# Scattering layer 2's expert results by token instead of gathering them by slot

## The reference

```
xn = _layernorm(x, axis=-1)
s = _L2_attn_ref(xn, ...)
g = _silu(_L2_ffn_ref(xn, ...))
x = x + s * g

def _L2_ffn_ref(x, ...):            # 32 experts, 4 for each token, H = 128
    scores = jax.nn.softmax(logits, axis=-1)
    topk_scores, topk_idx = jax.lax.top_k(scores, TOPK)
    topk_scores = topk_scores / jnp.clip(topk_scores.sum(axis=-1, keepdims=True), 1e-12, None)
    h = jax.nn.silu(jnp.einsum('nd,ehd->neh', flat, gate_w)) * jnp.einsum('nd,ehd->neh', flat, up_w)
    expert_out = jnp.einsum('neh,edh->ned', h, down_w)
    sel = jnp.take_along_axis(expert_out, topk_idx[:, :, None], axis=1)
    out = (sel * topk_scores.astype(flat.dtype)[:, :, None]).sum(axis=1)
    out = out + jax.nn.silu(flat @ sgate_w.T) * (flat @ sup_w.T) @ sdown_w.T
```

## Time and profile before

| | |
|---|---|
| median of 3 runs | 3026.65 us (3012.79 to 3027.65) |
| profiled execution | 3031.52 us |
| its span, first to last instruction | 3029.9 us |
| mean granted clock of PE | 0.854 of full speed |
| busy: PE, DVE, ACT, POOL | 2294.3, 1649.9, 1244.2, 726.5 us |
| layer 2's expert tiles, first row load to the next block | 2323.8 to 2505.55 us |
| `between_layers` | 2505.55 to about 2790 us |
| layer 3's `linear_attention` and projection | 2826.2 to 2890.4 us |
| layer 3's expert tiles, `finish` | 2890.4 to the end |

### The profile page before, as it was taken

How to read it: one execution, slowest core, us unless ns; L and a number is a source line. 1 busy time by engine, 2 the same in 40 slices (tenths; PEclk the granted TensorE clock), 3 DMA queues, 4 the chain that set the end, 5 groups by cost and what they waited for, 6 DMA issues and landing times. The chain is left out here.

```text
span 3029.9 us, 44630 instructions
## 1 busy us (share of the span) xinstructions
PE 2294.3 (76%) x15583; PEld 1330.6 (44%) x15600; DVE 1649.9 (54%) x3303; ACT 1244.2 (41%) x1898; POOL 726.5 (24%) x874
## 2 busy tenths in 40 slices
PE   3487788883599999989750399999998884776486
PEld 1255555552334444444340134444444772344275
DVE  2467676761187756657138277777772441544202
ACT  0234444422156656566520046555665440232043
POOL 0143434443010101100000132323221116450423
PEclk9588898886699999999855599999998996796588
DMA  9000000002002111110000302121212991110065
GB/s 258 1 2 2 2 2 2 2 2 64 31 14 61 35 43 31 56 27 27 1 1 11 92 25 75 48 70 48 70 52 94 314 303 49 31 37 3 28 225 179
DMA packets 135515, 183.14 MB, mean 60 GB/s; under 512 B 26329, under 2 KB 108458, under 8 KB 130190
## 3 DMA queue, kind: packets, MB, share of 16 engines
q1 hardware_dynamic: 95235, 135.53, 15.1%
q0 software_dynamic: 13696, 32.02, 3.3%
q10 hardware_dynamic: 26400, 13.13, 1.5%
HBM read 127.86 MB, written 52.21 MB: 59 GB/s over the span
## 5 line engine op out<-in xcount | busy, mean ns | idle before, releaser
L1691 DVE TENSOR_REDUCE a_mpart<-a_mx 128x1 f32<-128x512 f32 (+3 forms) x1216 | 741.8, 657 | 293.3 <-PE a_mx L1462 157.1
L1605 ACT ACTIVATE a_prob<-a_st 128x1024 f32<-128x1024 f32 (+3 forms) x768 | 607.5, 812 | 489.8 <-PE a_st L1488 367.1
L1462 PE MATMUL a_mx<-a_ka,a_qa 96*128 96x512 bf16 (+3 forms) x1536 | 429.2, 339 | 33.8 <-DVE a_mpart L1691 17.0
L1485 PE MATMUL a_st<-a_qa,a_ka 96*128 96x512 bf16 (+3 forms) x1536 | 416.5, 334 | 27.2 <-ACT a_prob L1605 21.4
L1503 PE MATMUL a_acc<-a_prob,a_v_aug 128*9 128x512 f32 (+3 forms) x3072 | 323.5, 497 | 0.0
L1462 PEld LDWEIGHTS a_mx<-a_ka,a_qa 96*128 96x128 bf16 x1536 | 141.3, 99 | 321.4 <-DVE a_mpart L1691 174.1
L1389 POOL DMA_INDIRECT x_rows<-l_xn,l_slots x128 | 125.5, 980 | 403.5 <-ACT a_prob L1605 393.5
L1488 PE MATMUL a_st<-w_mask_t,identb 128*128 128x128 bf16 x1024 | 208.3, 223 | 0.0
L1485 PEld LDWEIGHTS a_st<-a_qa,a_ka 96*128 96x128 bf16 x1536 | 146.1, 99 | 132.8 <-ACT a_prob L1605 37.4
L2053 PE MATMUL t_psu<-t_xsT,t_w 128*128 128x128 f32 x960 | 149.5, 290 | 22.9 <-DMA t_w<-in_l_experts 13.4
L1465 PE MATMUL a_mx<-w_mask_q,identb 128*128 128x128 bf16 x768 | 164.8, 224 | 0.0
(11 more groups left out here) (451 smaller groups left out, 4115.8 us busy)
## 6 DMA issues: line engine op xcount, KB each, us to landing
t_w<-in_l_experts SPq DMA_DIRECT2D x160, 192.0 KB, 4.0
t_w<-in_l_experts SPq DMA_DIRECT2D x40, 514.0 KB
a_qa<-q_parts_dram SPq DMA_DIRECT2D x96, 192.0 KB
a_ka<-k_parts_dram SPq DMA_DIRECT2D x96, 192.0 KB
x_rows<-zeros SPq DMA_DIRECT2D x25, 512.0 KB, 6.7
t_xs<-x_rows ACTq DMA_DIRECT2D x40, 256.0 KB, 4.2
y_rows<-t_y POOLq DMA_DIRECT2D x40, 256.0 KB
q_parts_dram<-a_parts SPq DMA_DIRECT2D x24, 256.0 KB
```

What stands on the lines that cost most here:

```text
L1462: ins = pe.matmul(to, qa[G % NQ][:, h0 + k, qi * P:(qi + 1) * P], ka[G % NQ][:, h0 + k, lo:hi], start=not masked_first, stop=k == per - 1 ...
L1485: ins = pe.matmul(to[:, lo:HALF], ka[G % NQ][:, h, j * P:(j + 1) * P], qa[G % NQ][:, h, ch * HALF + lo:(ch + 1) * HALF], start=True, stop= ...
L1605: act.activation(prob[:, v % NP_, 2 * pair:2 * pair + 2, lo:HALF], sring[s % 2][:, :, lo:HALF], ACT.Exp, scale=1.0 if alibi else scale).th ...
L1691: dve.tensor_reduce(mpart[:, G % 2, h0:h0 + per, qi, piece], slot[:, 0:per * width].rearrange("p (k w) -> p k w", k=per), X, ALU.max).then ...
```

## The change

Row numbers travel with layer 2's rows, too. `x2_rows` gets the column D, `y2_rows` is laid out by token (row 4 * token + k) with 160 tiles of spare rows behind it for unused slots. The expert tiles of layer 2 scatter each tile's results to these rows as those of layer 3 do, four indirect DMAs a half; the number copies of both layers go from DVE to POOL, one half ahead of the half's scatters, into a tile that holds the numbers of all tiles; ACT's loads of rows stand one tile before the end of a half and wait for that copy. The attention of layer 2 adds 1 to the numbers on POOL before the scatters of k = 1, 2, 3 of each sequence. `between_layers` reads the four results of a token as 2 KB in a row, by 16 plain DMAs of SP, 512 KB each, in place of 128 gathers. The projection of the last sequence moves into the block of its attention. The cores of the parts:

```diff
-                        sp.dma_start(x3_rows.rearrange("(i p) d -> p i d", p=P)[:, :, D], row_id[:], allow_slow_non_contiguous=True
-                                     ).then_inc(ids_filled, 16)
                         sp.wait_ge(loaded, 16 * len(loads))
+                        for rows, ids in zip((x2_rows, x3_rows), no_token):
+                            sp.dma_start(rows.rearrange("(i p) d -> p i d", p=P)[:, :, D], ids[:], allow_slow_non_contiguous=True
+                                         ).then_inc(ids_filled, 16)
...
+                            if k and t == 0:
+                                ids = seqs[b].rows[:, :, D]
+                                pool.wait_ge(placed[b], 16 * NT * k)
+                                pool.tensor_scalar(ids, ids, 1.0, None, ALU.add).then_inc(numbered, 1)
+                                pool.wait_ge(numbered, (TOPK - 1) * b + k)
                             pool.indirect_dma_start(x2_rows, bass.IndirectOffsetOnAxis(x_slots[:, k, b * NT + t:b * NT + t + 1], 0),
-                                                    seqs[b].xn[:, t], None, bounds_check=x2_rows.shape[0] - 1).then_inc(placed[b], 16)
+                                                    seqs[b].rows[:, t], None, bounds_check=x2_rows.shape[0] - 1).then_inc(placed[b], 16)
...
+                    def keep_ids(it, half):
+                        at = it * body + half * hb
+                        pool.wait_ge(x_loaded[half], 16 * (it + 1))
+                        pool.tensor_copy(ids[:, at:at + hb], xs[:, half, :, D]).then_inc(ids_kept, 1)
+
                     def store(it, half):
                         pool.wait_ge(y_out, it * pairs + (half + 1) * hb // 2)
-                        if base is None:
-                            pool.dma_start(half_tiles(y_view, it, half), y[:, half]).then_inc(y_stored[half], 16)
-                        else:
-                            for j in range(hb):
-                                pool.indirect_dma_start(y_rows, bass.IndirectOffsetOnAxis(ids[:, half, j:j + 1], 0), y[:, half, j], None,
-                                                        bounds_check=y_rows.shape[0] - 1).then_inc(y_stored[half], 16)
-
-                    if base is None:
-                        with pool.Fori(0, iters) as it:
-                            for half in range(2):
-                                store(it, half)
-                    else:
-                        for it in range(iters):
-                            for half in range(2):
-                                pool.wait_ge(ids_kept, 2 * it + half + 1)
-                                store(it, half)
+                        pool.wait_ge(ids_kept, 2 * it + half + 1)
+                        for j in range(hb):
+                            at = it * body + half * hb + j
+                            pool.indirect_dma_start(y_rows, bass.IndirectOffsetOnAxis(ids[:, at:at + 1], 0), y[:, half, j], None,
+                                                    bounds_check=y_rows.shape[0] - 1).then_inc(y_stored[half], 16)
+
+                    for half in range(2):
+                        keep_ids(0, half)
+                    for it in range(iters):
+                        for half in range(2):
+                            if it + 1 < iters:
+                                keep_ids(it + 1, half)
+                            store(it, half)
...
-                            if ahead and base is not None and k % hb == hb - 1:
+                            if ahead and k % hb == hb - 2:
                                 act.wait_ge(ids_kept, 2 * it + k // hb + 1)
                                 load(it + 1, k // hb)
...
-                    def keep_ids(it, half):
-                        wait(dve, y_stored[half], it * stores)
-                        dve.wait_ge(x_loaded[half], 16 * (it + 1))
-                        dve.tensor_copy(ids[:, half], xs[:, half, :, D]).then_inc(ids_kept, 1)
...
-                    sp.wait_ge(ids_filled, 16)
+                    view = y2_rows[0:TOPK * BATCH * T].rearrange("(b t p k) d -> b p t (k d)", b=BATCH, p=P, k=TOPK)
+                    for e in order:
+                        if e[0] == "gather":
+                            _, b, q = e
+                            if at[e] >= NB:
+                                sp.wait_ge(summed, at[e] - NB + 1)
+                            sp.dma_start(back[:, at[e] % NB], view[b, :, tiles_of(q)]).then_inc(back_s[at[e] % NB], 16)
 
                 @block.gpsimd
                 def _(pool):
                     pool.memset(v[:, :, D:D + 1], 1.0).then_inc(ones_s, 1)
-                    for e in order:
-                        if e[0] == "gather":
-                            _, b, q = e
-                            k_at = at[e]
-                            if k_at >= NB:
-                                pool.wait_ge(summed, k_at - NB + 1)
-                            for t in range(PER):
-                                for k in range(TOPK):
-                                    fetch(pool, back[:, k_at % NB, k, t], y2_rows, slots[:, k], b * NT + q * PER + t, back_s[k_at % NB])
```

```diff
+                    pe.wait_ge(y_out, NT // 2)
+                    for t in range(NT):
+                        ins = pe.transpose(psq[:, t * P:(t + 1) * P], att[:, t], ident[:])
+                    ins.then_inc(out_turned, 1)
+                    pe.wait_ge(out_kept, 1)
+                    for t in range(NT):
+                        pe.matmul(psq[:, t * P:(t + 1) * P], attT[:, t * P:(t + 1) * P], W["l3_wo"][:], start=True, stop=False)
+                        ins = pe.matmul(psq[:, t * P:(t + 1) * P], ones3[:], B["l3_bo"], start=False, stop=True)
+                        if t % (NT // 2) == NT // 2 - 1:
+                            ins.then_inc(out_made, 1)
...
+                    act.wait_ge(out_turned, 1)
+                    act.copy(attT[:], psq[:]).then_inc(out_kept, 1)
+                    for half in range(2):
+                        act.wait_ge(out_made, half + 1)
+                        act.copy(q.s_att[:, half * NT // 2:(half + 1) * NT // 2], psq[:, half * HALF:(half + 1) * HALF].rearrange(
+                            "p (t d) -> p t d", d=D))
```

251 lines of the change are left out of this document (107 added, 144 removed).

## The result

The changed kernel took **3142.51 us** (median of 4 runs, 3135.27 to 3145.94) against 3027.15 us (3012.79 to 3028.08) for the kernel before: **1.0389 [1.0353, 1.0425] times as long**. The forecast was 3023.4, 0.1% less than before, with a range up to 3064; the kernel became 3.9% slower.

| stage | before | after | change | forecast |
|---|---|---|---|---|
| `prepare` | 80.4 | 113.1 | +32.6 | +0.5 |
| layer 2's four `layer_norm` blocks | 32.6 | 56.0 | +23.4 | 0 |
| layer 2's expert tiles | 181.0 | 331.5 | +150.5 | +77.8 |
| `between_layers` | 286.1 | 210.1 | -76.0 | -70.4 |
| `linear_attention` to layer 3's first load | 64.2 | 52.0 | -12.2 | -13.1 |

The account below looks back on a forecast made before the run. In layer 2's expert tiles DMA was at 0.98, with POOL to become the bound. 3031.5 (profiled execution) +77.8 -70.4 -13.1 +2 +0.5 = 3028.3, so 3023.4 beside the median; range 2992 to 3064 us.

Parts of the forecast that it names:

- Layer 2's tiles: Layer 2's expert tiles: 160 scatters for 40 stores lengthen an iteration from 8.38 to 12.1 us, +77.8 us.
- Neither binds at this pace: Layer 2's tiles: neither DVE's wait for landed scatters nor the load's wait for POOL's number copy delays the iteration.
- The prediction's test: Layer 2's tiles: POOL waits for DVE's `y` some 5 us if POOL is the bound, 20 or more if PE is.
- fourth rival: Layer 2's tiles: numbers come too late, so loads wait for POOL's copies; a mechanism within the first two rivals, no own chance.
- The step from 44 matmuls under 10.24 us of scatters, and 12 more in 1.8 us, to 12.1 us: Layer 2's tiles: PE's 56 matmuls an iteration pass at 4.3 a microsecond beside scatters, the rest at 6.6.
- the serialised rival: Layer 2's tiles: PE's results arrive only behind each burst of four scatters, 13.4 us an iteration, 3049 us; chance 0.25.
- POOL alone: Layer 2's tiles: POOL is the only bound, 11.04 us an iteration, 56.6 for 77.8, 3002 us; chance 0.33.
- main reading: `between_layers`: what happens beside POOL's gathers, PE and ACT running late, goes with them; -70.4 us in sum.
- terms (2) to (4): `between_layers`: sequence 0's turning -5.7 and normalisation wait -5.0, its slow-clock projection -7.2, ACT's late copies after output projections -11.9.
- The rival in which the gaps stay: `between_layers`: gathers didn't cause the gaps, which stay, while layer 2's tiles cost 11.04 us an iteration; 3073 us, chance 0.08.
- Joined projection: End of `linear_attention`: the last projection ends under the scatters or within a few us; -13.1 us, -5 if cover were gone.
- Fill of the numbers: First layer-norm block of layer 2: two non-contiguous SP DMAs instead of one, hidden by the routing; 0, at worst 5 us.

Follow-up runs that it names:

- second run of spaced gathers: Kernel before with the joined projection alone, plus a small POOL memset ahead of each of the 128 gathers between the layers; 2958.84 us.

## Why the prediction was wrong, point by point

**Layer 2's tiles, the term that failed most.** It was +77.8 at 12.1 us an iteration and measured +150.5 at 15.6. Two steps failed.
- The step "the next rows' load waits for the number copy, which POOL makes one half ahead. Neither binds at this pace." It bound. The load went from its early place to the end of a half, so rows that used to lie ready came late: T 10.50 with late loads and number copies against 8.24 without, both with plain stores. The prediction counted when POOL would make the copy and not when the rows behind it would land. Load, landing, copy and the next load form a ring. POOL's 75.8 us of waiting for rows show the ring but aren't its price, since with the copy behind the scatters that wait went to DVE's results at nearly the same T. The prediction's test, POOL's wait for DVE's `y`, looked at another releaser (8.2 us in the same window). Its fourth rival, "loads wait for POOL's copies", is this mechanism, and it was given no price and no chance.
- The step from 44 matmuls under 10.24 us of scatters, and 12 more in 1.8 us, to 12.1 us. In the iteration shown above 37 pass in 11 us, and the other 21 take 5 us, at a granted clock of 0.50. The pace of 4.3 a microsecond was itself misread: it divides 24 matmuls by the 5.59 us until ACT began, while PE's own rows there end at 2845.19, 3.1 us after the first. The other 2.5 us are the hold-up; in a run without it ACT began 3.13 us after the first of these matmuls (2777.88 and 2781.01, the second run of spaced gathers). Hold-ups were real in the condition of the result, but their size was the serialised rival's, whose worst case, "up to 16 us an iteration and 3100", nearly names 15.6. Its condition, a fallen clock, is there (0.77 over the window above), and its reason, that PE has no work ahead to cover the hold-ups, fits rows that come late; no run tests that.

The two losses aren't a sum that holds everywhere: scatters add 5.1 us to late loads where the hold-ups are, and 0.5 where they are not (11.02 and 10.50, the latter measured where hold-ups were). What scatters cost behind early loads wasn't run; it would need the numbers from elsewhere than the loaded rows.

**Rival "POOL alone", 11.04 us.** Wrong for the run that counted. In the condition without hold-ups the number is right within 0.02 us, in part by luck, as said.

**Between the layers.** -70.4 forecast, -76.0 measured. Its main reading holds: with 128 gathers that nobody reads the stage took 60 us more, and PE's matmuls went one by one again. The terms (2) to (4) weren't tested one by one. The rival in which the gaps stay is refuted. The rule that spoke for it (the Trainium skill, "SBUF — State Buffer", section "SBUF: two separate sides", PE and ACT never wait on anyone) disagrees with 269.7 against 210.1 us as far as the prediction applied it, to all that holds PE and ACT, and agrees with the other condition, 212.7 us with the gathers in place. Whether what holds them there has to do with SBUF, no run shows. A gain read from one execution was thus a gain in one condition: in the other this part of the change gives 2 to 6 us (212.7, 215.6 and 216.5 with gathers, 210.8 without).

**Joined projection.** -13.1 forecast, -12.2 measured, and 52 us in each kernel that joins it. The projection ends under the scatters, as forecast; layer 3's load leaves 5.3 us after the last of them has been issued. Less 2.1 for landing that is 3.2 us, where the prediction named 2.4 or less: the term was right but for this. After, ACT's last copy of the projection, POOL's last scatter, ACT's first load of rows:

```profile
2986.54 0.59 ACT L2538 COPY l_s_att<-a_psq 128x512 f32<-128x512 f32 x1 [3.17 <-issue]
```

```profile
2993.01 0.97 POOL L1917 DMA_INDIRECT x_rows<-l_xn,l_slots  x1 [0.30 <-issue]
```

```profile
2999.26 0.96 ACTq L2070 DMA_DIRECT2D t_xs<-x_rows  x2
```

By itself, with all else as before, it isn't clear of no change (0.9979 [0.9956, 1.0002]); 12 us would be 0.996, which the interval holds too.

**Fill of the rows, taken as 0.** The step "Rows of 516 instead of 512 bytes ... 0" was right for loads and wrong for the fill: 78.5 us for 45.1. The prediction priced the layout where it is read and not where it is first written: 20 of the 25 stores of 512 KB have 512-byte pieces that now lie 516 apart, as those of layer 3's five did before. `prepare` ended 32.6 us later. It has no row of SP in that stage, where these stores stood back to back over 45.08 of 80.4 us: there was little slack for a slower one.

**Fill of the numbers, "0, at worst 5".** +23.4. "What hides them is the routing" was said of their landing, and the issue was forgotten: 20480 single words and behind them 5120 held SP's queue 28.8 us, and a block ends only when SP's program has. Of this the issue of the second, smaller fill took 28.39 us; by itself, before, it took 0.40. It was held behind the first, so what a fill of 20480 words alone would have cost wasn't run. The issue, not the landing, was the price.

**Attention, +2.** Not measurable: layer 2's attention took 655.1 us for 660.9, and 653 to 661 over all kernels. The two attention stages, of which the first isn't touched, gave 9.1 us to the changed kernel here; within that spread it can't be called the change's work.

So the sum, which put the profiled execution at 3028.3, missed it by 114.7 us: 72.7 in layer 2's tiles, 32.6 and 23.4 in the two fills, less 14.0 in the other terms. Without the fills' 56 us the forecast would still have been 59 us off.

**What stays open.** What of an indirect DMA holds PE and ACT, and why one set of runs has it and another not; why eight scatters an iteration cost ten times what four beside plain stores do; whether spaced gathers are harmless; what scatters cost behind early loads; and why PE's chain in `prepare` ends 16 us later in some executions.

## What to carry to other kernels

When data that steers a DMA travels inside the rows of a load, follow the whole ring (load, landing, copy, use, next load) and ask how far ahead it still runs, not only whether each engine has time. Price a new row width at every writer, initial fills among them, and count the issue time of what stands behind a many-element DMA in its queue against the end of the block. A gain that consists of vanished hold-ups is worth only what the hold-ups cost in the condition at hand, so time the kernel before again beside each set.

## What the runs showed of the hardware

- **Two conditions.** The same kernel before took 3025 to 3040 us in four sets of runs, the result's among them, and 2957 to 2959 in two, with one chip among both. The stage between the layers alone, with its gathers as before, was 286 to 293 us in the one and 213 to 217 in the other: about the whole difference. In the hold-up, 41 to 47 of 64 small matmuls still pass at full pace (the earlier trace rows and above), then most wait another 1.0 to 2.4 us each. It isn't a late load of instructions: the trace's records of those DMA queues have one of 16 KB 3.39 us after the first of these matmuls in the kernel before, and 3.30 in the joined one without hold-ups, 0.88 us long in both, and none while the matmuls pass one by one.
- **Writes of 512-byte pieces 516 bytes apart** ran at 161 GB/s (161 to 193 over the traces), those 512 apart at 294, and runs of 4128 bytes at 407. Loads of rows of 516 bytes cost nothing that shows (T 8.24).
- **Single words:** a DMA of 20480 of them on SP and one of 5120 behind it took 28.8 us to issue, 28.39 of it the second, and landed after 34.8 and 41.4 us. The one of 5120 alone was issued in 0.40.
- **POOL's 0.30 us between two indirect DMAs** can hold a memset of 0.11 us at no cost.
